# Projecting the next key and value ahead of the second pair's scores, in every unit of an attention stage

## The chip, the core and the metric

The kernel runs on one core of one Trainium2 chip. The metric is device time in microseconds (us) of one execution, from the kernel's start to its end. The kernel before takes 1142.35 us, the median of three runs (1141.11 to 1142.4).

## What is computed

Eight sequences of 128 tokens with 512 features each go through three small layers with residual sums (a linear layer with a low-rank adapter, a layer with a weight chosen for each sequence, a low-rank layer), and then through attention with 32 query heads and 8 key/value heads of size 128. A group of four query heads shares one key head. The keys are 512 cached rows, gathered through a page table, followed by the 128 new ones. The attention part, cut to what matters:

```python
q = rope(rmsnorm(x @ Wq.T, q_norm_w), pos)      # 32 heads of 128
k = rope(rmsnorm(x @ Wk.T, k_norm_w), pos)      # 8 heads of 128
v = x @ Wv.T
k_all = concatenate([k_cache[block_table], k])  # 512 + 128 keys
v_all = concatenate([v_cache[block_table], v])
scores = where(valid, (q @ k_all.T) * SCALE, -1e30)
o = softmax(scores) @ v_all
return x + o @ Wo.T
```

All of it is float32. Most products are made of three faster ones, high times high, high times low and low times high, so for most tiles there is a `_hi` and a `_lo` half.

## The kernel before

The first stage (about the first 120 us) does the three small layers. The second, which the change touches, has 64 **units**: unit u is one key/value head with one sequence, that is four query heads of 128 rows against 640 keys. Each engine has its own program, written by hand, in which `step(n, ...)` is what it does in round n. A loop runs over most rounds (`Fori`), and the first two and the last stand unrolled. There is no scheduler. An engine does its instructions in the order written and waits on semaphores (`wait_ge`).

Round n mixes three units:

- **TensorE** (PE; `step`, from L1060): the scores of heads 0 and 1 of unit n (`score_pair(n, 0)`, which waits for `qt_lo_out` and `kc_lo_out`), the queries of unit n+1 (`project_queries`, into ps_q), the scores of heads 2 and 3 (`score_pair(n, 1)`), the new key and value of unit n+1 (`project_new_key`, into ps_kv), the output product of unit n-2 (`put_out`), the turned cached keys of unit n+1 (`turn_cached`), its turned queries and new key (`turn_rotated`, which waits for `q_summed` and `key_scaled`), and the products with the values of unit n-1 (`values`, which waits for `pt_in`).
- **VectorE** (DVE; `step`, L1342): for each head the row minimum of the negated scores (`lowest`, line L1315, which waits for `scores`), then 1/sum (`inverse`), the turn of the probabilities in blocks of 32 (`turn_blocks`, L1339), and for unit n+1 the rotary products of the queries (`rotate_queries`, L1257 and L1262), the variances (`variances`, L1270, which waits for `sq_done` and `vn_out`), the rotated key (`rotate_key`, L1277 to L1282), and at the end the low halves (`cached_low`, `rotated_low`, L1236).
- **ScalarE** (ACT; `step`, L785): the exponentials (`exps`, L767), the scaling by 1/sum (`normalize`, L772), the squares of the next queries and key (`query_squares`, `key_squares`, L723), the next value's copy (`new_value`, L720 v_next), the scaled key (`scale_key`, L741, which waits for `key_summed` and for `rstd_done`), the high halves, and two of the four transfers that place the turned probabilities (`place_rest`, L280).
- **GpSimd** (POOL): it adds the query's two rotary products (`sum_queries`), raises the variances to the power -1/2 (`norm_factors`, L548), and gathers the next cached keys (L528 k_raw, once `turn_cached` is done) and values.
- **The queue of SyncE** (SP): it sends the turned probabilities of heads 0 and 1 and then those of heads 2 and 3 to memory (`send_blocks`, blocks_placed<-blocks), reads half of them back in another order (`place_rows`, prob_t<-blocks_placed), and loads the next input (`next_input`, x_s, which waits for `kv_proj`) and weights.

The probabilities thus go round a loop: turned on VectorE, sent by SP, placed by SP and ScalarE (`place_rest(n - 1)` stands in ScalarE's `step` ahead of `exps(n, 0)` and waits until both sends of unit n-1 have landed: `act.wait_ge(blocks_out, 32 * (n + 1))` in L775), and then used by `values`.

Of the kernel before, what the change touches and what calls it, by code (L numbers as in the profile page):

```python
# [50 lines left out]
def build(nc, x, x_t, ids0, ids1, ids2, table, lens, w0_t, bias0, lora_a, lora_b, w1_t, w2_b, w2_a,  # L51
          w_qkvo, q_norm, k_norm, k_rows, v_rows, inv_freq, row_in_table, ident_in, out):
    ctx = ExitStack()
    with ctx:
# [60 lines left out]
        with ExitStack() as p1:  # L115
# [81 lines left out]
            def one(t, at):  # L197

                return t[bass.ds(at, 1)].rearrange("a p k r -> p (a k) r") if len(t.shape) == 4 else t[bass.ds(at, 1)].rearrange("a p c -> (a p) c")
# [3 lines left out]
        with ExitStack() as p2:  # L203
# [94 lines left out]
            with nc.Block() as block:  # L298
# [308 lines left out]
                def _(act):  # L607
# [62 lines left out]
                    def store(e):  # L670
                        act.wait_ge(t3_lo, e + 1)
                        act.dma_start(one(xt_dram, e), x3t[:, :, :].bitcast(F32)).then_inc(xt_stored, 16)
# [60 lines left out]
                    def key_squares(u):  # L733
                        act.wait_ge(kv_proj, u + 1)
                        square(ps_kv[:, 0:D], GROUP)

                    def scale_key(u):

                        act.wait_ge(key_summed, u + 1)
                        act.wait_ge(rstd_done, u + 1)  # L740
                        nc.scalar.activation(rot[:, GROUP, :], key_sum[:, :], ACT.Copy, scale=rstd[:, GROUP:GROUP + 1]).then_inc(key_scaled, 1)  # L741
# [23 lines left out]
                    def exps(n, h):  # L765
                        act.wait_ge(low_done, GROUP * n + h + 1)
                        nc.scalar.activation(prob[:, h, :], prob[:, h, :], ACT.Exp, bias=low[:, h:h + 1], scale=-1.0,  # L767
                                             accum_out=total[:, h:h + 1]).then_inc(exp_done, 1)
# [16 lines left out]
                    def step(n, last, head=True, out=True, first=False, third=False):  # L785
                        if head:
                            out_high(n - 2, 1, first=first)
                        if out:
                            place_rest(n - 1, first=not head)
                        exps(n, 0)  # L790
                        exps(n, 1)
                        normalize(n, 0)
                        normalize(n, 1)
                        if not last:
                            query_squares(n + 1, range(GROUP))
                            key_squares(n + 1)
                            new_value(n + 1, first=not out)
                        if third:
                            third_turned(B - 1)
                            store(B - 1)  # L800
                        exps(n, 2)
                        exps(n, 3)
                        if not last:
                            scale_key(n + 1)
                        normalize(n, 2)
                        normalize(n, 3)
                        if not last:
                            cached_high(n + 1, first=not out)
                            rotated_high(n + 1)
                        if last:  # L810
                            keep_turned(0, 0, 1)
                            keep_turned(0, 2, 3)
                        if out:
                            out_high(n - 1, 0, first=not head)
# [26 lines left out]
                def _(pe):  # L841
# [105 lines left out]
                    def project_queries(u, first=False):  # L947
                        pe.wait_ge(x_s_in, 16 * (u + 1))
                        if not first:
                            pe.wait_ge(w_split, ((u >> 3) << 3) + B)  # L950
                            pe.wait_ge(qt_lo_out, u)
                        project(ps_q[:, :], u, 0, GROUP * D).then_inc(q_proj, 1)

                    def project_new_key(u, first=False):

                        if not first:
                            pe.wait_ge(vn_out, u)
                        project(ps_kv[:, 0:2 * D], u, GROUP * D, 2 * D).then_inc(kv_proj, 1)
# [16 lines left out]
                    def score_pair(n, pair):  # L975


                        pe.wait_ge(low_done, GROUP * n + 2 * pair)
                        heads = 2 * pair, 2 * pair + 1

                        def part(h, piece):
                            lo, hi = CUTS[h % 2][piece]
                            q = qt_hi[:, h * P:(h + 1) * P], qt_lo[:, h * P:(h + 1) * P]
                            return three(ps_s[:, score_slot(h) + lo:score_slot(h) + hi], q,
                                         (keys_of(kt_hi, n, lo, hi), keys_of(kt_lo, n, lo, hi)), True, True)

                        for h in heads:
                            part(h, 0)
                        for h in heads:
                            part(h, 1).then_inc(scores, 1)  # L990
# [69 lines left out]
                    def step(n, last, out=True, pv=True, third=False):  # L1060
                        pe.wait_ge(qt_lo_out, n + 1)
                        pe.wait_ge(kc_lo_out, n + 1)
                        score_pair(n, 0)
                        if third:
                            layer_2_out(B - 1, slot(B - 1))
                        if not last:
                            project_queries(n + 1)
                        score_pair(n, 1)
                        if third:
                            third_turn(B - 1)  # L1070
                        if not last:
                            project_new_key(n + 1)
                        if out:
                            put_out(n - 2)
                        if not last:
                            turn_cached(n + 1)
                            turn_rotated(n + 1)
                        if last:
                            turn_last(0)
                        if pv:  # L1080
                            values(n - 1, first=not out, beside=last)
# [37 lines left out]
                def _(dve):  # L1119
# [47 lines left out]
                    def keep_sum(e):  # L1167
                        dve.wait_ge(x3_out, e + 1)
                        nc.vector.tensor_copy(y[:, bass.ds(e, 1), :].rearrange("p a c -> p (a c)"), x3[:, :]).then_inc(y_out, 1)
# [172 lines left out]
                    def step(n, weights, last, head=True, out=True, first=False):  # L1342
                        if head:
                            out_low(n - 2, 1)
                        dve.wait_ge(mask_set, n + 1)
                        dve.wait_ge(gain_done, n + 1)
                        if not first:
                            dve.wait_ge(blocks_turned, GROUP * n)
                        lowest(n, 0)
                        lowest(n, 1)  # L1350
                        if weights:
                            weights_high(n)
                        inverse(n, 0)
                        inverse(n, 1)
                        if not last:
                            rotate_queries(n + 1)
                            rotate_queries_rest(n + 1)
                        if first:
                            third_sum(B - 1, slot(B - 1))
                            keep_sum(B - 1)  # L1360
                        lowest(n, 2)
                        lowest(n, 3)
                        if first:
                            third_turned(B - 1)
                        if not last:
                            turn_blocks(n, 0, first)
                            variances(n + 1)
                            rotate_key(n + 1)
                            turn_blocks(n, 1)
                        inverse(n, 2)  # L1370
                        inverse(n, 3)
                        if head:
                            add_out(n - 2)
                        if last:
                            keep_turned(0, 1, 2)
                        else:
                            turn_blocks(n, 2)
                            turn_blocks(n, 3)
                            cached_low(n + 1)
                            rotated_low(n + 1)  # L1380
                            gains(n + 1)
                        if out:
                            out_low(n - 1, 0)
                        if not last:
                            dve.wait_ge(low_done, GROUP * (n + 1))
                            set_mask(n + 1)
# [116 lines left out]
```

## Time and profile before

| | |
|---|---|
| time, median of 3 runs | 1142.35 us |
| lowest, highest | 1141.11, 1142.4 us |
| the profiled execution, its own time | 1145.5 us |
| its span, from first to last instruction | 1143.8 us |
| TensorE busy | 1109.5 us (97% of the span) |
| VectorE busy | 867.5 us (76%) |
| ScalarE busy | 697.3 us (61%) |
| GpSimd busy | 478.8 us (42%) |
| mean granted TensorE clock | 0.991 of full speed |

The profile is of one execution. Times of rows are us from the span's start, and durations of groups are means. TensorE's matmuls overlap, so the distance from one start to the next says what one costs. "[0.21 <-issue]" behind a row says that the engine sat idle for 0.21 us before it and waited for nothing that the profile shows; another name there is the instruction whose end released it. SPq, ACTq and POOLq are the engines as issuers of transfers.

### The profile page before, as it was taken

What the parts mean: (1) busy time and instruction counts of PE and PEld (TensorE: products, weight loads), DVE (VectorE), ACT (ScalarE), POOL (GpSimd) and SP (SyncE); (2) the same over time, 40 slices, a digit from 0 to 9 for tenths busy, and PEclk for the clock granted to TensorE, in tenths of its full rate; (3) what the DMA queues carried; (4) which work ended last, traced back from release to release, by engine and by line L of the source; (5) the groups of instructions that cost most, each with busy time, mean ns of one, the idle gap of its engine ahead of it and who ended that gap; (6) DMA issues with size and microseconds to landing.
All of it is one profiled execution on the core that took longest, in us unless ns stands there. A gap on an engine that the chain in (4) does not pass through costs nothing.

```text
span 1143.8 us, 27449 instructions
## 1 busy us (share of the span) xinstructions
PE 1109.5 (97%) x6116; PEld 972.0 (85%) x6116; DVE 867.5 (76%) x2203; ACT 697.3 (61%) x1949; POOL 478.8 (42%) x570
## 2 busy tenths in 40 slices
PE   5999699999999999999999999999999999999998
PEld 3656588888888889898898988989888888889886
DVE  3568778877787877778777887778877788777773
ACT  2344556766666666666666676666766666666663
POOL 6855334444344444344443444444444444432330
PEclk9999899999999999999999999999999999999999
DMA  6694577887778878787887887877888878777883
GB/s 180 211 310 164 176 233 252 260 256 242 256 246 270 254 235 259 246 273 248 243 255 247 266 251 249 252 255 252 259 252 246 255 254 264 234 222 227 245 249 99
DMA packets 125331, 275.77 MB, mean 241 GB/s; under 512 B 14076, under 2 KB 78716, under 8 KB 124290
## 3 DMA queue, kind: packets, MB, share of 16 engines
q1 hardware_dynamic: 78736, 193.37, 48.7%
q10 hardware_dynamic: 35426, 45.49, 16.1%
q0 software_dynamic: 11152, 36.72, 12.3%
q8 instruction: 6, 0.10, 0.0%
q14 instruction: 11, 0.09, 0.0%
HBM read 186.67 MB, written 88.87 MB: 241 GB/s over the span
## 4 chain that ended last, share of the span: by engine, by line
PE 85%; DMA 4%; DVE 1%; ACT 1%; issue 1%; POOL 0%; ACTq 0%; SPq 0%; DVEq 0%; POOLq 0%
PE ps_o L1008 23%; PE ps_q L943 15%; PE ps_kv L943 8%; PE ps_s L853 6%; PE ps_s L851 6%; PE ps_s L852 6%; PE ps_o L852 5%; PE ps_o L851 5%; PE ps_o L853 5%; DMA prob_t<-blocks_placed 2%; PE ps_q L972 2%; PE ps_x L964 2%; DMA blocks_placed<-blocks 2%; PE ps_kv L973 1%; DVE blocks L1339 1%
## 5 line engine op out<-in xcount | busy, mean ns | idle before, releaser
L767 ACT ACTIVATE prob<-prob,low 128x640 f32<-128x640 f32 x256 | 210.3, 827 | 156.8 <-DVE low L1315 148.3
L1315 DVE CUSTOM_DVE_ANT_0 prob<-ps_s,mask,q_gain 128x640 f32<-128x640 f32 x256 | 215.5, 879 | 34.3 <-PE ps_s L853 34.1
L1008 PE MATMUL ps_o<-prob_t,v_raw 128*128 128x256 f32 x992 | 236.0, 381 | 0.6 <-DMA prob_t<-blocks_placed 0.4
L1339 DVE STREAM_TRANSPOSE blocks<-prob 128x640 f32<-128x640 f32 x252 | 204.1, 829 | 1.8 <-ACT prob L772 1.8
L1008 PEld LDWEIGHTS ps_o<-prob_t,v_raw 128*128 128x128 f32 x992 | 184.5, 191 | 23.8 <-issue 1.0
L772 ACT ACTIVATE prob<-prob,inv 128x640 f32<-128x640 f32 x256 | 196.5, 815 | 0.0
L851 PE MATMUL ps_s<-kt_hi,qt_hi 128*128 (+1 forms) x512 | 171.1, 334 | 3.8 <-DVE kt_lo L1236 2.3
L943 PE MATMUL ps_q<-w_hi,x_s 128*128 (+1 forms) x512 | 171.5, 395 | 0.0
L853 PE MATMUL ps_s<-kt_hi,qt_lo 128*128 (+1 forms) x512 | 159.5, 311 | 0.0
L852 PE MATMUL ps_s<-kt_lo,qt_hi 128*128 (+1 forms) x512 | 159.0, 311 | 0.0
L720 ACT ACTIVATE ot_hi<-ps_o 128x256 fp32r<-128x256 f32 x128 | 49.0, 383 | 162.3 <-PE ps_o L1008 155.5
L108 POOL TENSOR_TENSOR w_lo<-w_raw,w_hi 128x640 f32 (+1 forms) x64 | 101.1, 1580 | 97.2 <-DVE w_hi L102 96.0
L1236 DVE TENSOR_TENSOR ot_lo<-ps_o,ot_hi 128x256 fp32r<-128x256 f32 x128 | 53.6, 419 | 84.5 <-ACT ot_hi L720 84.3
L544 POOL TENSOR_TENSOR rot<-rot_a,rot_b 128x512 f32<-128x512 f32 x64 | 82.8, 1293 | 81.6 <-DVE rot_b L1262 81.6
L943 PEld LDWEIGHTS ps_q<-w_hi,x_s 128*128 128x128 f32 x512 | 96.2, 188 | 20.7
L548 POOL TENSOR_TENSOR rstd<-var,neg_half 128x5 f32<-128x5 f32 x64 | 77.0, 1203 | 69.6 <-DVE var L1270 69.6
L851 PEld LDWEIGHTS ps_s<-kt_hi,qt_hi 128*128 128x128 f32 x512 | 96.9, 189 | 9.3 <-DVE kt_lo L1236 2.7
L943 PE MATMUL ps_q<-w_lo,x_s 128*128 (+1 forms) x256 | 101.1, 395 | 0.0
L852 PEld LDWEIGHTS ps_s<-kt_lo,qt_hi 128*128 128x128 f32 x512 | 97.1, 190 | 4.6
L943 PE MATMUL ps_kv<-w_hi,x_s 128*128 (+1 forms) x512 | 101.0, 281 | 0.0
L555 POOL COPY v_new<-v_next 128x128 f32 (+1 forms) x64 | 18.4, 288 | 192.7 <-PE ps_o L1008 177.2
L852 PE MATMUL ps_o<-w_lo,ot_hi 128*128 (+1 forms) x252 | 98.8, 392 | 0.0
(194 smaller groups left out, 2256.2 us busy)
## 6 DMA issues: line engine op xcount, KB each, us to landing
blocks_placed<-blocks SPq DMA_DIRECT2D x126, 640.0 KB, 3.9
prob_t<-blocks_placed ACTq DMA_DIRECT2D x126, 320.0 KB, 5.6
prob_t<-blocks_placed SPq DMA_DIRECT2D x126, 320.0 KB, 6.4
x_s<-xt_split SPq DMA_DIRECT2D x64, 512.0 KB, 3.7
w_raw<-w_qkvo_dram SPq DMA_DIRECT2D x55, 320.0 KB, 3.8
w<-w_t_dram SPq DMA_DIRECT2D x8, 1024.0 KB, 6.8
xt_split<-x3t ACTq DMA_DIRECT2D x8, 512.0 KB, 5.3
w_raw<-w_qkvo_dram POOLq DMA_DIRECT2D x9, 320.0 KB, 6.3
```

Of the source, the lines that this page charges most:

```text
L108: return nc.gpsimd.tensor_tensor(lo, raw, hi.bitcast(F32), ALU.subtract)
L544: nc.gpsimd.tensor_tensor(rot[:, 0:GROUP, :], rot_a[:, 0:GROUP, :], rot_b[:, 0:GROUP, :], ALU.add).then_inc(q_summed, 1)
L548: nc.gpsimd.tensor_tensor(rstd[:, :], var[:, :], neg_half[:, :], ALU.pow).then_inc(rstd_done, 1)
L767: nc.scalar.activation(prob[:, h, :], prob[:, h, :], ACT.Exp, bias=low[:, h:h + 1], scale=-1.0, accum_out=total[:, h:h + 1]).then_inc(exp_ ...
L772: nc.scalar.activation(prob[:, h, :], prob[:, h, :], ACT.Copy, scale=inv[:, h:h + 1]).then_inc(prob_done, 1)
L851: nc.tensor.matmul(dst, lh, rh, start=first, stop=False)
L852: nc.tensor.matmul(dst, lh, rl, start=False, stop=False)
L853: return nc.tensor.matmul(dst, ll, rh, start=False, stop=final)
L943: mm = nc.tensor.matmul(dst, x_s[:, int(i % 3 == 2), k * P:(k + 1) * P], w_rest if i % 3 == 1 else w, start=i == 0, stop=i == 3 * KT - 1)
L1008: mm = nc.tensor.matmul(ps_o[pair][:, 0:PAIR], v, turned_probs(c, pair), start=c == 0, stop=c == CH - 1)
L1315: nc.vector.tensor_tensor_reduce(out=prob[:, h, :], in0=ps_s[:, score_slot(h):score_slot(h) + KEYS], in1=mask[:, :], scale=q_gain[:, h:h + ...
L1339: nc.vector.transpose(blocks[:, h // 2, :, :, h % 2, :].rearrange("p j c q -> p c j q"), prob[:, h, :].rearrange("p (c j k) -> p c j k", c ...
```

## The change

No instruction is added or removed. In every unit that has a next one, three pieces move:

- TensorE: `project_new_key(n + 1)` stands ahead of `score_pair(n, 1)`, where it stood behind it.
- VectorE: `turn_blocks(n, 0)`, `variances(n + 1)` and `rotate_key(n + 1)` stand ahead of `lowest(n, 2)` and `lowest(n, 3)`.
- ScalarE: `scale_key(n + 1)` stands ahead of `exps(n, 2)` and `exps(n, 3)`.

```diff
@@ scalar, step @@
+                        if not last:
+                            scale_key(n + 1)
                         exps(n, 2)
                         exps(n, 3)
-                        if not last:
-                            scale_key(n + 1)
                         normalize(n, 2)
                         normalize(n, 3)
@@ tensor, step @@
                             project_queries(n + 1)
+                        if not last:
+                            project_new_key(n + 1)
                         score_pair(n, 1)
                         if third:
                             third_turn(B - 1)
-                        if not last:
-                            project_new_key(n + 1)
                         if out:
                             put_out(n - 2)
@@ vector, step @@
+                        if not last:
+                            turn_blocks(n, 0, first)
+                            variances(n + 1)
+                            rotate_key(n + 1)
                         lowest(n, 2)
                         lowest(n, 3)
                         if first:
                             third_turned(B - 1)
                         if not last:
-                            turn_blocks(n, 0, first)
-                            variances(n + 1)
-                            rotate_key(n + 1)
                             turn_blocks(n, 1)
                         inverse(n, 2)
                         inverse(n, 3)
```

VectorE's instructions in the middle of one unit (the second, which stands unrolled; the loop has the same order), from the rotary products of the queries on. The two pairs of ISA rows are `lowest` of heads 2 and 3. Before:

```order
L1257 TENSOR_TENSOR rot_a<-ps_q,cos_q 128x512
L1262 TENSOR_TENSOR rot_b<-ps_q,sin_q 128x4x64 x2
L1315 ISA prob,low<-ps_s,mask,q_gain 128x640
L1315 ISA low 128x1
L1315 ISA prob,low<-ps_s,mask,q_gain 128x640
L1315 ISA low 128x1
L1339 STREAM_TRANSPOSE blocks<-prob 128x5x4x32
L1270 TENSOR_SCALAR var<-sq 128x5
L1277 TENSOR_TENSOR rot_a<-ps_kv,cos_k 128x128
L1279 TENSOR_TENSOR rot_b<-ps_kv,sin_k 128x64 x2
L1282 TENSOR_TENSOR key_sum<-rot_a,rot_b 128x128
L1339 STREAM_TRANSPOSE blocks<-prob 128x5x4x32
```

And with the change:

```order
L1257 TENSOR_TENSOR rot_a<-ps_q,cos_q 128x512
L1262 TENSOR_TENSOR rot_b<-ps_q,sin_q 128x4x64 x2
L1339 STREAM_TRANSPOSE blocks<-prob 128x5x4x32
L1270 TENSOR_SCALAR var<-sq 128x5
L1277 TENSOR_TENSOR rot_a<-ps_kv,cos_k 128x128
L1279 TENSOR_TENSOR rot_b<-ps_kv,sin_k 128x64 x2
L1282 TENSOR_TENSOR key_sum<-rot_a,rot_b 128x128
L1315 ISA prob,low<-ps_s,mask,q_gain 128x640
L1315 ISA low 128x1
L1315 ISA prob,low<-ps_s,mask,q_gain 128x640
L1315 ISA low 128x1
L1339 STREAM_TRANSPOSE blocks<-prob 128x5x4x32
```

The transpose of head 0, the variances and the four instructions of the key moved from behind the two `lowest` to ahead of them.

ScalarE's instructions in the same unit, from the key's square to the scaling of heads 2 and 3; "x2" are the two heads. The difference, with - for before and + for the change:

```order
 L723 ACTIVATE junk,sq<-ps_kv 128x128
 L720 ACTIVATE v_next<-ps_kv 128x128
+L741 ACTIVATE rot<-key_sum,rstd 128x128
 L767 ACTIVATE prob,total<-prob,low 128x640 x2
-L741 ACTIVATE rot<-key_sum,rstd 128x128
 L772 ACTIVATE prob<-prob,inv 128x640 x2
```

The scaled key moved from behind the exponentials of heads 2 and 3 to ahead of them.

## Rows read from the trace of the kernel before

**Rows 1.** Busy time per stretch: stretch and length; PE, PEld, DVE, ACT, POOL; clock, DMA

```profile
608.09:623.89 15.80, 15.80 (x91) 14.19 (x90) 12.56 (x33) 10.21 (x29) 6.71 (x8) 1.00 0.80 249
200.00:1050.00 850.00, 850.00 (x4787) 762.79 (x4786) 675.97 (x1775) 550.96 (x1565) 353.79 (x425) 1.00 0.80 251
```

**Rows 2.** Timeline of TensorE, unit from 608.09: start us, us, engine, line, operation

```profile
612.84 0.28 PE L851 MATMUL ps_s<-kt_hi,qt_hi 128*128 x1
...
614.62 0.28 PE L943 MATMUL ps_kv<-w_hi,x_s 128*128 x1
```

**Rows 3.** Timeline of VectorE, the same unit

```profile
613.42 0.69 DVE L1257 TENSOR_TENSOR rot_a<-ps_q,cos_q 128x512 f32<-128x512 f32 x1 [0.21 <-issue]
614.02 0.74 DVE L1262 TENSOR_TENSOR rot_b<-ps_q,sin_q 128x256 f32<-128x256 f32 x2
614.69 0.87 DVE L1315 CUSTOM_DVE_ANT_0 prob<-ps_s,mask,q_gain 128x640 f32<-128x640 f32 x1
...
616.29 0.84 DVE L1339 STREAM_TRANSPOSE blocks<-prob 128x640 f32<-128x640 f32 x1
...
617.10 0.28 DVE L1277 TENSOR_TENSOR rot_a<-ps_kv,cos_k 128x128 f32<-128x128 f32 x1
...
617.67 0.29 DVE L1282 TENSOR_TENSOR key_sum<-rot_a,rot_b 128x128 f32<-128x128 f32 x1
...
619.17 0.69 DVE L1332 TENSOR_TENSOR y<-ps_o,y 128x512 f32 x1 [0.34 <-PE ps_o L853]
619.78 1.56 DVE L1339 STREAM_TRANSPOSE blocks<-prob 128x640 f32<-128x640 f32 x2
...
622.43 0.27 DVE L1236 TENSOR_TENSOR kt_lo<-ps_kv,kt_hi 128x128 f32 x1
```

**Rows 4.** Timeline of ScalarE, the same unit

```profile
610.30 0.85 ACTq L280 DMA_DIRECT2D prob_t<-blocks_placed  x2
...
614.88 0.28 ACT L723 ACTIVATE junk<-ps_q 128x128 f32<-128x128 f32 x1 [0.42 <-DVE rot_b L1262]
...
616.24 0.28 ACT L723 ACTIVATE junk<-ps_kv 128x128 f32<-128x128 f32 x1 [0.21 <-PE ps_kv L943]
...
616.50 0.27 ACT L720 ACTIVATE v_next<-ps_kv 128x128 f32 x1
616.66 0.83 ACT L767 ACTIVATE prob<-prob,low 128x640 f32<-128x640 f32 x1
...
617.47 0.83 ACT L767 ACTIVATE prob<-prob,low 128x640 f32<-128x640 f32 x1
...
618.87 1.53 ACT L772 ACTIVATE prob<-prob,inv 128x640 f32<-128x640 f32 x2
```

**Rows 5.** Timeline, POOL and ACTq, same unit; then transfers issued from 621.1 to 621.6

```profile
617.26 1.20 POOL L548 TENSOR_TENSOR rstd<-var,neg_half 128x5 f32<-128x5 f32 x1 [1.03 <-DVE var L1270]
...
620.64 1.05 POOL L528 DMA_INDIRECT k_raw<-k_rows_dram,k_row  x1 [0.79 <-POOL k_row L525]
...
626.19 0.85 ACTq L280 DMA_DIRECT2D prob_t<-blocks_placed  x2
...
blocks_placed<-blocks SPq DMA_DIRECT2D x1, 640.0 KB, 4.7
```

**Rows 6.** Unit 1: key gather, second send, and that send's us to landing

```profile
143.49 1.05 POOL L528 DMA_INDIRECT k_raw<-k_rows_dram,k_row  x1 [0.79 <-POOL k_row L525]
...
145.45 0.33 SPq L275 DMA_DIRECT2D blocks_placed<-blocks  x1
...
blocks_placed<-blocks SPq DMA_DIRECT2D x1, 640.0 KB, 3.7
```

**Rows 7.** Transfers issued from 998.1 to 998.5, us to landing last: a first send

```profile
blocks_placed<-blocks SPq DMA_DIRECT2D x1, 640.0 KB, 3.0
```

**Rows 8.** Timeline of TensorE and VectorE, unit from 892.66: scores begin; queries are rotated

```profile
892.66 0.47 PE L851 MATMUL ps_s<-kt_hi,qt_hi 128*128 x1
...
897.81 0.69 DVE L1257 TENSOR_TENSOR rot_a<-ps_q,cos_q 128x512 f32<-128x512 f32 x1 [0.56 <-PE ps_q L943]
```

## The prediction, made before the changed kernel ran

> **What bounds the kernel now.** Read the busy time by stretch first [rows 1]. From 200 to 1050 us TensorE is busy for all of the 850 us, at the full granted clock, and VectorE for 676. The unit that I follow starts its scores at 608.09 and the next at 623.89. It is 15.80 us long, and TensorE is busy for all of it. The 18 units from there to 892.66 [rows 8] give 15.81 us each. So TensorE sets the time, and an order that lets the others be ready sooner can give nothing back there. The question is only whether TensorE is made to wait. That is read from the timelines of the other engines, as the distance from their last step to TensorE's need.
>
> Two such distances matter. The first: VectorE ends the last low half, which `score_pair(n+1, 0)` waits for, at 622.43 + 0.27 = 622.70 [rows 3], and TensorE needs it at 623.89, so 1.19 us are to spare. The second is less visible. ScalarE issues `place_rest` at 610.30 [rows 4] and at 626.19 [rows 5], each time when the second send of the unit before has landed, and its first exponential of the unit stands behind that issue. From these exponentials come the inverses of heads 0 and 1, and `rotate_queries` stands behind those on VectorE: it starts at 613.42, 3.12 us after the issue, and its 0.21 us of idleness before has no release by TensorE [rows 3]. So a loop runs through ScalarE, VectorE and a transfer: place, exponentials, queries rotated, ... head 3 turned, sent, landed, place. The loop is kept in step by TensorE at one point only: the square of the key waits 0.21 us for `project_new_key` [rows 4].
>
> **The change part by part.** I count from R, the start of `rotate_queries`, and put each later step beside what it was.
>
> TensorE: the same matmuls in another order. The scores of the second pair take 614.62 - 612.84 = 1.78 us [rows 2], so the key and value are ready 1.78 us sooner, and the second pair's scores later by the shorter key projection. By itself that costs TensorE nothing. The key's square no longer waits. It then follows the query squares, which is 0.2 to 0.35 us sooner, because those began at R + 1.46 and did not move [rows 4]: I take R + 2.5, before R + 2.82. The one point at which TensorE kept the loop in step is gone.
>
> VectorE: after the query rotation it turns head 0 (0.84 us) and is then early. `variances` waits for the copy of the value, which ScalarE makes behind the squares: R + 2.5 + 0.26 + 0.27 = R + 3.03 [rows 4]. Behind this wait stand the key's rotation and now both `lowest`. After a short wait the register work of a dynamic address shows, as 0.21 us did for the queries [rows 3], so the key's rotation starts at R + 3.24, its sum 0.57 us later [rows 3] and `lowest(n, 2)` about 0.2 us behind that, at R + 4.0. Before, it was at 614.69, which is R + 1.27. **The second pair's minima start 2.7 us later**; the scores are there long before.
>
> ScalarE: `lowest` takes 0.87 and its result is read just behind, so `exps(n, 2)` starts at R + 4.93 where it was at 616.66, R + 3.24. The new order on ScalarE gives about the same moment by another way: GpSimd's power starts 0.16 us after the key's rotation (617.10 to 617.26) and takes 1.20 us [rows 3, 5], so to R + 4.6, and the scaled key comes between it and the exponential, some 0.4 us. So `scale_key` ahead of the exponentials adds next to nothing more. 1.7 us are lost here, since before the exponential had waited for the squares anyhow. Then: `exps(n, 3)` 0.81 later at R + 5.74; the scaling of head 2 at R + 6.6 and of head 3 at R + 7.36, ended at R + 8.17 (before 618.87 + 1.53, R + 6.98) [rows 4].
>
> VectorE again: `inverse(n, 3)` waits for the exponential of head 3, to R + 6.7, and behind it stands `add_out`, with some 0.3 us of instruction and registers ahead of it: R + 7.0. From there 0.61 to the transposes and 1.56 for both [rows 3]: **head 3 is turned at R + 9.17**, before 621.34, R + 7.92. The last low half ends 622.70 - 621.34 = 1.36 later, R + 10.53, and TensorE can start at R + 10.65 with the 0.12 us that ScalarE needs after VectorE's end (614.76 to 614.88). Before it started at R + 10.47. Against an R that does not move that is 0.18 us too late.
>
> Two lengths follow. **TensorE and VectorE alone:** R cannot be sooner than 5.15 us after the unit's first score, which is where it starts when it does wait for TensorE (892.66 to 897.81) [rows 8]. 5.15 + 10.65 = 15.80: just what a unit is now. **The loop through the transfer:** 3.12 from place to R, 9.17 to head 3 turned, L for the send's landing, and 0.15 for the steps at its two ends (626.19 - 621.34 - 4.7), together 12.44 + L. At L = 4.7 as now [rows 5] that is 17.14. The same steps before are 626.19 - 610.30 = 15.89, with the key's wait of 0.21 among them: without the wait 15.68, so the loop was just under a unit's length.
>
> **What L will be** is the one unknown. The second send shares the transfer engines with the gather of the cached keys, issued at 620.64, 0.7 us before head 3 is turned (621.34), and lands in 4.7 us [rows 5]. In unit 1 the gather was issued 145.45 - 143.49 = 1.96 us ahead of the send, and it landed in 3.7 [rows 6]. A send with nothing beside it lands in 3.0 [rows 7]. Both ends are kept: 3.0 gives 15.44, which is under TensorE's own 15.80, and 4.7 gives 17.14. The gather hangs on TensorE's turn, 620.64 - 608.09 = 12.55 us after the unit's first score. With a unit of 16.14 us the place is issued 16.14 - 3.12 - 10.65 = 2.37 after the first score and the second send 3.12 + 9.17 + 0.07 after that, at 14.7: 2.2 us behind the gather. That is nearest to rows 6, so I take L = 3.7, and the unit is **16.14 us**.
>
> The Trainium skill ("DMA: Bandwidth & Descriptors", Anatomy of one DMA) gives a transfer about 2.0 us fixed and its bytes over 436 GB/s, which for 640 KB is an estimate of 3.5 us; by it the unit would be 15.94 and the kernel 1150 us. The trace disagrees for a send alone: 3.0 [rows 7].
>
> The sum: units 2 to 61 run in this loop, 60 of them. 60 x (16.14 - 15.81) = 19.8 us. Against the profiled execution's own 1145.5 us that is 1165; against the median of the runs, 1142.35, it is 1162. What the other side gives is small: the wait of `turn_rotated` for the key scaled falls away, at most the 0.01 us by which 15.81 is over 15.80, 0.6 us in all. `next_input` and the next weights are issued some 1.8 us sooner, while the probabilities are being placed. SP's own two placements stand ahead of them in its queue, so I take nothing; if they did delay the last placement, that would be in the upper part of the range.
>
> **Rivals.**
> 1. *Not slower: the send has the engines to itself.* If L is 3.3 or less, 12.44 + L is under 15.8, the loop has slack again, and R falls back to 5.15, at which the other length is 15.80. Then the time is 1142 (1140 to 1144). For it: the gather is moved 1.5 us further ahead of the send, and 3.0 was seen [rows 7]. Against it: the first send now goes out beside the gather and both push work toward the second, and in rows 6 1.96 us were not enough.
> 2. *The send lands in 3.3 to 3.6 us.* Unit 15.8 to 16.04, time 1143 to 1156. This is where the skill's figure, DMA: Bandwidth & Descriptors, would put it.
> 3. *L stays 4.4 to 4.7.* The unit is 16.84 to 17.14 us, the time 60 x 1.03 to 1.33 more, 1204 to 1222. For it: nearly every unit of the trace shows it. Against it: each shows it at the same distance from the gather, which the change moves.
> 4. *Faster*: only if waits at TensorE that I priced at 0.6 us were larger. Nothing in rows 1 allows it.
>
> **How the numbers follow.** Forecast, L of 3.6 to 4.3 and a time of 1156 to 1200: 0.45, likeliest 1162. Rival 1: 0.21. Rival 2: 0.16. Rival 3: 0.12. Rival 4: 0.03. The remaining 0.03 are slower in a way I do not name. A measurement of this kernel can tell about 0.2% (2.3 us) from no change. So slower has 0.76, the same 0.21 and faster 0.03. The range from 1142 to 1200 holds the forecast, rival 2 and most of rival 1, about 8 in 10, and leaves out rival 3.
>
> **What would show it.** In the profile after, units are 16.0 to 16.4 us apart, and TensorE has a gap before the scores of each (ps_s L851, released by kt_lo L1236), where before it had none. `lowest(n, 2)` starts 4.0 us after `rotate_queries` instead of 1.27, with about 1 us of idle VectorE ahead of the variances, released by v_next. The first exponential of a unit still follows the place issue directly, and the second send lands in 3.6 to 4.3 us. Wrong would be: no gap ahead of the scores and a second send of about 3.0 us (rival 1), or a chain from R to the last low half that is not near 10.5 us.

## The result, and the profile with the change

The kernel with the change takes **1154.47 us** (median of six runs, 1151.77 to 1158.59). The kernel before took 1142.38 us beside it (median of six, 1141.11 to 1143.85). The ratio is 1.0111, with a 95% interval of 1.0091 to 1.0131, so it is 1.1% slower. The profiled execution took 1158.59 us, the longest of the six, with a span of 1156.9 us.

Times below are medians, and "unit" is the distance from one unit's first score to the next, between 200 and 1050 us. Before it is 15.81 us in 49 of 52 units. Now 44 of 52 are 15.96 to 16.00, the median is 15.97, four take 16.20 to 16.28, and the mean is 16.00. 60 units by 0.19 are 11.4 us, nearly all of the 12.1 us.

Busy time of one typical unit and of the long stretch; the columns are those of [rows 1], which it answers:

```profile
615.56:631.53 15.97, 15.97 (x91) 14.06 (x90) 12.85 (x35) 10.00 (x29) 6.69 (x8) 1.00 0.79 249
200.00:1050.00 850.00, 849.09 (x4730) 747.47 (x4731) 680.15 (x1749) 530.23 (x1538) 351.31 (x424) 1.00 0.78 248
```

By the busy time TensorE still looks full, since the record of a matmul is longer than the distance to the next start. The last one of the products with the values starts at 631.21 and is shown for 0.38 us, over the whole gap ahead of the next scores. The wait shows in the idle time of the weight load ahead of the scores (20.0 us in 54 units, in the list of waits below, where the kernel before has none) and in the distances between starts. The timeline of TensorE in the same unit (first score; first key and value matmul; scores of the second pair; the last two matmuls of the values; the next unit's first score):

```profile
615.56 0.38 PE L851 MATMUL ps_s<-kt_hi,qt_hi 128*128 x1
...
620.22 0.28 PE L943 MATMUL ps_kv<-w_hi,x_s 128*128 x1
...
621.59 0.28 PE L851 MATMUL ps_s<-kt_hi,qt_hi 128*128 x1
...
630.99 0.59 PE L1008 MATMUL ps_o<-prob_t,v_new 128*128 128x256 f32 x2
631.53 0.38 PE L851 MATMUL ps_s<-kt_hi,qt_hi 128*128 x1
```

VectorE in that unit, answering [rows 3]. The number behind "idle" in brackets is the idle time just before the row:

```profile
620.62 0.69 DVE L1257 TENSOR_TENSOR rot_a<-ps_q,cos_q 128x512 f32<-128x512 f32 x1 [0.27 <-PE ps_q L943]
...
621.89 0.83 DVE L1339 STREAM_TRANSPOSE blocks<-prob 128x640 f32<-128x640 f32 x1
623.74 0.17 DVE L1270 TENSOR_SCALAR var<-sq 128x5 f32<-128x5 f32 x1 [1.01 <-ACT junk L723]
623.87 0.29 DVE L1277 TENSOR_TENSOR rot_a<-ps_kv,cos_k 128x128 f32<-128x128 f32 x1
...
624.67 0.88 DVE L1315 CUSTOM_DVE_ANT_0 prob<-ps_s,mask,q_gain 128x640 f32<-128x640 f32 x1
...
628.25 1.56 DVE L1339 STREAM_TRANSPOSE blocks<-prob 128x640 f32<-128x640 f32 x2
...
630.90 0.28 DVE L1236 TENSOR_TENSOR kt_lo<-ps_kv,kt_hi 128x128 f32 x1
```

ScalarE, answering [rows 4]: the placement, the key's square, the scaled key, and the exponential and the scaling of the second pair:

```profile
617.45 0.85 ACTq L280 DMA_DIRECT2D prob_t<-blocks_placed  x2
...
623.10 0.29 ACT L723 ACTIVATE junk<-ps_kv 128x128 f32<-128x128 f32 x1
...
625.28 0.40 ACT L741 ACTIVATE rot<-key_sum,rstd 128x128 f32<-128x128 f32 x1 [1.64 <-POOL rstd L548]
625.59 0.82 ACT L767 ACTIVATE prob<-prob,low 128x640 f32<-128x640 f32 x1
...
627.23 1.53 ACT L772 ACTIVATE prob<-prob,inv 128x640 f32<-128x640 f32 x2
```

The cached keys' gather, the second send and the placement behind it, answering [rows 5, 6]; they come from the timelines of POOL, SP and ACTq:

```profile
627.98 1.05 POOL L528 DMA_INDIRECT k_raw<-k_rows_dram,k_row  x1 [0.79 <-POOL k_row L525]
...
629.89 0.33 SPq L275 DMA_DIRECT2D blocks_placed<-blocks  x1
...
633.46 0.86 ACTq L280 DMA_DIRECT2D prob_t<-blocks_placed  x2
```

And what the engines waited for from 200 to 1050 us (us in total, times, longest):

```profile
ACT rot L741 <- POOL rstd L548: 86.8, 53, 1.6
...
DVE var L1270 <- ACT junk L723: 53.9, 53, 1.0
...
PEld ps_s L851 <- issue: 20.0, 54, 0.7
DVE rot_a L1257 <- PE ps_q L943: 12.8, 45, 0.4
```

Two things are to be seen. The first is a new idle microsecond of VectorE ahead of the variances, in each of 53 units, with both minima behind it. The second is the line on ps_q: in 45 of 53 units the rotation of the queries now waits for TensorE, where before it did so in 12. A TensorE that starts its unit late is itself what starts the next long chain late.

### The profile page after: what moved, and what is told of

Same layout as the page of the kernel before. It is cut to its first block and busy times, and to the rows that moved or that the text cites. A ratio compares the mean times of both kernels' runs of the same rounds, so it can differ in the third digit from the quotient of the medians.

```text
span 1156.9 us, 27449 instructions
## 1 busy us (share of the span) xinstructions
PE 1118.7 (97%) x6116; PEld 964.2 (83%) x6116; DVE 885.9 (77%) x2203; ACT 684.7 (59%) x1949; POOL 480.0 (41%) x570
## 5 line engine op out<-in xcount | busy, mean ns | idle before, releaser
L851 PE MATMUL ps_s<-kt_hi,qt_hi 128*128 (+1 forms) x512 | 165.9, 324 | 7.1 <-DVE kt_lo L1236 4.5
L853 PE MATMUL ps_o<-w_hi,ot_lo 128*128 (+1 forms) x252 | 99.5, 395 | 0.0
L943 PE MATMUL ps_kv<-w_hi,x_s 128*128 (+1 forms) x512 | 98.3, 277 | 0.0
L851 PE MATMUL ps_o<-w_hi,ot_hi 128*128 (+1 forms) x252 | 98.1, 389 | 0.0
```

Source lines behind the costliest of these rows:

```text
L851: nc.tensor.matmul(dst, lh, rh, start=first, stop=False)
L853: return nc.tensor.matmul(dst, ll, rh, start=False, stop=final)
L943: mm = nc.tensor.matmul(dst, x_s[:, int(i % 3 == 2), k * P:(k + 1) * P], w_rest if i % 3 == 1 else w, start=i == 0, stop=i == 3 * KT - 1)
```

## The experiments

The distances between the first matmuls of TensorE's pieces tell where a unit is lost. They are medians between 200 and 1050 us, and each ends at the next piece in the order of that kernel. "Scores" without a number are those of heads 0 and 1, "scores 2" those of heads 2 and 3.

| us | before | after | key scaled last | TensorE alone | TensorE undone | one minimum first |
|---|---|---|---|---|---|---|
| scores to queries | 1.946 | 1.860 | 1.946 | 1.946 | 1.858 | 1.946 |
| queries | 2.800 | 2.800 | 2.800 | 2.800 | 2.800 | 2.800 |
| key and value | 1.413 | 1.372 | 1.372 | 1.372 | 1.413 | 1.372 |
| scores 2 | 1.787 | 1.766 | 1.766 | 1.766 | 1.787 | 1.766 |
| output product | 2.748 | 2.764 | 2.764 | 2.764 | 2.748 | 2.764 |
| turned cached keys, to turned queries | 0.435 | 0.435 | **1.635** | **1.446** | 0.435 | 0.435 |
| turned queries and key, to values | 0.546 | 0.546 | 0.573 | 0.574 | 0.546 | 0.546 |
| values, to next scores | 4.132 | **4.426** | 4.132 | 4.132 | **4.879** | 4.132 |
| mean unit | 15.81 | 16.00 | 16.99 | 16.80 | 16.48 | 15.77 |

### Each part alone

**The scaled key put back behind the exponentials**, with the rest of the change kept:

```diff
-if not last:
-    scale_key(n + 1)
 exps(n, 2)
 exps(n, 3)
+if not last:
+    scale_key(n + 1)
```

> The changed kernel with ScalarE's part alone undone: scale_key stands behind exps(n, 2) and exps(n, 3) again. Theory A (the chain behind the wait for the value's copy, and each engine's place in it, sets the unit): the exponentials do not start sooner, since the minima are not ready before 10.0 us after the unit's first score; the scaled key comes behind them, at about 12.0 instead of 10.1, and turn_rotated on TensorE, which needs it at 11.0, waits for it: unit about 16.9 us, time about 1205 (1190 to 1215). Rival (VectorE's new order alone costs time, ScalarE's place is neutral): 1154, as with the change.

It took 1215.76 us, 1.0647 (1.062 to 1.0674) of the kernel before. The size of theory A was right to 1%, the time just above its range. TensorE's turned queries wait, since the new key that is turned with them comes last on ScalarE:

```profile
620.12 0.39 ACT L741 ACTIVATE rot<-key_sum,rstd 128x128 f32<-128x128 f32 x1
...
620.65 0.63 PE L972 MATMUL ps_q<-ident,rot 128*128 128x128 f32 x4 [1.04 <-ACT rot L741]
```

So the third part of the change is what makes the second one bearable: it is worth some 60 us here.

**TensorE's part alone** on the kernel before:

```diff
+if not last:
+    project_new_key(n + 1)
 score_pair(n, 1)
 if third:
     third_turn(B - 1)
-if not last:
-    project_new_key(n + 1)
```

> The kernel before with TensorE's part alone: project_new_key ahead of score_pair(n, 1), VectorE and ScalarE as before. Theory A: the scores of heads 2 and 3 come 1.4 us later, lowest(n, 2) waits for them to 7.7 us after the first score instead of 6.6, and all that stands behind it, the variances and the key among it, is 1.1 us later; the scaled key is ready at 12.0 where turn_rotated needs it at 11.1: unit about 16.9 us, time about 1207 (1190 to 1215). Rival (a move among matmuls on an engine that is always busy costs nothing by itself, as the prediction said): 1142.

It took 1200.28 us, 1.0513 (1.0486 to 1.0541). The rows of VectorE, POOL, ScalarE and TensorE in one unit:

```profile
622.54 0.88 DVE L1315 CUSTOM_DVE_ANT_0 prob<-ps_s,mask,q_gain 128x640 f32<-128x640 f32 x1 [1.17 <-PE ps_s L853]
...
625.13 1.21 POOL L548 TENSOR_TENSOR rstd<-var,neg_half 128x5 f32<-128x5 f32 x1 [2.31 <-DVE var L1270]
...
626.43 0.40 ACT L741 ACTIVATE rot<-key_sum,rstd 128x128 f32<-128x128 f32 x1 [1.22 <-POOL rstd L548]
...
626.97 0.41 PE L972 MATMUL ps_q<-ident,rot 128*128 128x128 f32 x2 [0.85 <-ACT rot L741]
```

The minima wait for scores that now come 1.4 us later, and in the old order the variances stand behind them, and so on through GpSimd and ScalarE to TensorE. The sentence "by itself that costs TensorE nothing" in the prediction is wrong when the part stands alone: 1.0 us in each unit.

**TensorE's part undone**, with VectorE's and ScalarE's kept:

```diff
-if not last:
-    project_new_key(n + 1)
 score_pair(n, 1)
 if third:
     third_turn(B - 1)
+if not last:
+    project_new_key(n + 1)
```

> The changed kernel with TensorE's part alone undone: project_new_key stands behind score_pair(n, 1) again, VectorE and ScalarE as with the change. Theory A: the key's square waits for TensorE to 8.06 us after the first score instead of starting at 7.54, the value's copy and all behind it are 0.52 us later, so the unit grows from about 15.97 to about 16.5: time about 1184 (1176 to 1192). Rival (the loop through the transfer sets the unit, and VectorE's chain has slack): less than 0.1 us a unit, 1154 to 1160.

It took 1183.23 us, 1.037 (1.0342 to 1.0398), as theory A had it. VectorE's wait ahead of the variances is 1.52 us long instead of 1.01, and what is late at the end is the last low half, as a gap ahead of the scores:

```profile
616.46 0.17 DVE L1270 TENSOR_SCALAR var<-sq 128x5 f32<-128x5 f32 x1 [1.52 <-ACT junk L723]
...
624.24 0.38 PE L851 MATMUL ps_s<-kt_hi,qt_hi 128*128 x1 [0.40 <-DVE kt_lo L1236]
```

0.51 us more of this one wait made the median unit 0.50 us longer (16.47 against 15.97). That is the clearest evidence that the wait lies on the chain that sets the time.

### The wait filled

One `lowest` put into VectorE's idle microsecond, and one exponential into ScalarE's:

```diff
@@ vector @@
 turn_blocks(n, 0, first)
+lowest(n, 2)
 variances(n + 1)
 rotate_key(n + 1)
-lowest(n, 2)
 lowest(n, 3)
@@ scalar @@
-if not last:
-    scale_key(n + 1)
 exps(n, 2)
+if not last:
+    scale_key(n + 1)
 exps(n, 3)
```

> The changed kernel with lowest(n, 2) moved into VectorE's idle time, between turn_blocks(n, 0) and variances(n + 1), and scale_key between exps(n, 2) and exps(n, 3). Nothing else differs. Theory A (the loss is the wait for the value's copy with both minima queued behind it): head 2's minimum is taken while the copy is made, head 3 is turned near 13.6 us after the first score instead of 14.25, the last low half ends near 15.0 and TensorE does not wait: unit 15.80, time 1142 (1140 to 1145). Rival (the loop through the transfer sets the unit, since the second send again goes out close behind the gather of keys): 15.9 to 16.1, 1147 to 1158.

It took 1138.88 us (median of twelve), 0.998 (0.9961 to 1.0) of the kernel before, and 1.3% less than the change. VectorE waits 0.33 us for the scores and then not at all for the squares:

```profile
617.82:633.58 15.76, 15.76 (x91) 14.13 (x90) 12.78 (x34) 10.22 (x29) 6.69 (x8) 1.00 0.81 256
...
625.85 0.88 DVE L1315 CUSTOM_DVE_ANT_0 prob<-ps_s,mask,q_gain 128x640 f32<-128x640 f32 x1 [0.33 <-PE ps_s L853]
...
626.66 0.17 DVE L1270 TENSOR_SCALAR var<-sq 128x5 f32<-128x5 f32 x1
```

So taking one of the two minima out from behind the wait, with its exponential ahead of the scaled key, gives the whole loss back. The two moves were made together, and neither was tried alone. TensorE does not wait any more, and its unit is 15.76 us, 0.05 shorter than before. The table says why: key and value right behind the queries cost 0.041 us less, the second scores 0.021 less, the output product 0.016 more. 60 units by 0.05 are 3 us. Measured were 2.4 us against the kernel before beside it, in an interval that reaches from none to 4.5, so the gain in time is no more than likely. I had expected no gain (15.80).

### Which of two loops sets the unit

The prediction had two lengths: the chain through TensorE and VectorE, and the loop through the transfer. In the changed kernel the first is 15.97. For the second the typical unit has 12.44 + 3.43, which is 15.87, too near to tell them apart by the lengths. The start of the query rotation tells more. Where nothing else holds it, it follows the placement by 3.11 us. In 38 of 52 units it comes later than that, 3.13 to 3.30 us behind the placement, since VectorE waits for TensorE's queries there, and these units are set by the chain through TensorE. In the other 14 the placement is the last to come, or ties. The transfer loop passes ScalarE only because the placements stand ahead of its exponentials. If SP issues all four, it is cut. One wait had to be added to ScalarE's end, for all sends, ahead of the copies of the last unit's turned probabilities:

```diff
@@ sync, step @@
-for j in range(NB // 2):
+for j in range(NB):
     place_rows(sp, j)
@@ scalar, step @@
-if out:
-    place_rest(n - 1, first=not head)
@@ scalar, keep_turned @@
+act.wait_ge(blocks_out, 32 * (UNITS - 1))
```

> The changed kernel with all four placements of the turned probabilities issued by SP; ScalarE issues none, so its first exponential no longer stands behind the landing of the second send, and the loop through the transfer is cut. Theory A (the chain of TensorE, VectorE and ScalarE sets nearly every unit, 15.97 us, and the transfer only the few whose send is late): those few go, mean unit 16.00 to 15.97, time 1151 to 1154. Rival (the loop through the transfer sets the unit): it falls to 15.80 or near, time 1142 to 1146.

It took 1160.87 us, 1.0176 (1.0158 to 1.0195): both missed, theory A by 7 us. The waits from 200 to 1050 us:

```profile
DVE rot_a L1256 <- PE ps_q L942: 29.8, 53, 0.6
PEld ps_s L850 <- issue: 13.4, 40, 0.6
...
PEld ps_o L1007 <- issue: 4.7, 14, 0.6
PE ps_o L1007 <- DMA prob_t<-blocks_placed: 1.5, 5, 0.4
```

The queries' rotation now waits for TensorE in all 53 units, so the transfer loop is off it, and still 40 units have the gap ahead of the scores, with the median unit at 15.99. But SP's last two placements come later and the products with the values wait for them, a cost that the experiment added.

The same was then tried with the placements left on ScalarE, but behind the exponentials of heads 0 and 1:

```diff
-if out:
-    place_rest(n - 1, first=not head)
 exps(n, 0)
 exps(n, 1)
+if out:
+    place_rest(n - 1, first=not head)
```

> The changed kernel, with ScalarE's two placements of the turned probabilities issued behind the exponentials of heads 0 and 1 instead of ahead of them. The loop through the transfer then no longer passes through the exponentials, and has over 1 us to spare. Theory A (the chain TensorE and VectorE alone, 5.06 + 10.56 + 0.35 us, sets the unit): the typical unit stays 15.97 us, only the units with a late send get as short as the others, time 1152 (1150 to 1155). Rival (the loop through the transfer sets the unit, the gap ahead of the scores is only where it shows): the unit falls to 15.80 us, time 1142 to 1145. The placements are issued at 2.9 and 3.3 us after the unit's first score and land 6 us later, 1.5 us or more ahead of the products with the values.

It took 1160.23 us, 1.0165 (1.0132 to 1.0197). The time is out of both ranges. The units decide nevertheless: with the transfer loop cut, none is shorter than 15.96, and 19 of 52 are 15.96 or 15.97. The rival, 15.80, did not come about in a single unit. So the chain through TensorE and VectorE gives 15.97, and what is over it here is late placements again: the products with the values start 0.617 us on average behind the turned queries, where 0.546 is the undisturbed distance.

### The hidden loop in the kernel before

If the transfer loop was just under a unit before, a small copy on ScalarE, idle 39% of the time, must cost something when it stands in that loop. It adds a copy of 128x512 ahead of the unit's first exponential; nothing reads what it writes:

```diff
 if out:
     place_rest(n - 1, first=not head)
+copy(junk[:, 0:GROUP, :].rearrange("p h d -> p (h d)"), pos[:, :])
 exps(n, 0)
```

> The kernel before with one extra instruction a unit on ScalarE, a copy of 128x512 into a scratch tile, behind place_rest and ahead of exps(n, 0), about 0.5 us. ScalarE is busy for 61% of the time and TensorE for 97%. Theory A (a hidden loop through ScalarE, VectorE and the transfer runs just under the unit's length): the copy lengthens the way from the placement to rotate_queries by 0.5 us, the scaled key comes too late for turn_rotated, unit 15.9 to 16.25, time about 1157 (1148 to 1169). Rival (ScalarE has room): 1142.

It took 1155.19 us, 1.0127 (1.0104 to 1.015), theory A to 2 us. The mean unit is 15.99, and what waits is the turned queries, for the scaled key:

```profile
PEld ps_q L973 <- issue: 8.9, 29, 0.5
...
PE ps_q L973 <- ACT rot L741: 1.7, 8, 0.3
```

The copy lengthens the way from the placement to the rotation by 0.45 us (3.56 against 3.11). Some of it comes back, as the second send is now 0.98 us behind the gather and lands in 4.39 us instead of 4.56.

To show that its place in the loop is what costs, the loop was cut for it in the two ways from above. With SP issuing all placements:

> The kernel before with the same extra copy, and with all four placements issued by SP. Theory A: without the placement ahead of it the copy lies in ScalarE's idle time before the first minimum is ready (2.6 us after the first score), and the time is 1142 (1140 to 1145). Rival (the copy costs by itself, wherever the placement is): as the run before it.

It took 1157.84 us, 1.0132 (1.0109 to 1.0156). And with ScalarE's placements behind the exponentials:

> The kernel before with the same extra copy on ScalarE ahead of the unit's first exponential, and the two placements behind the exponentials of heads 0 and 1. Theory A (the extra copy cost 0.18 us a unit only because it stands in the loop through the transfer): unit back to 15.81 us, time 1142 (1140 to 1145). Rival (the copy costs by its time on ScalarE, wherever the placements stand): unit 15.99, time 1155 as with the copy alone.

It took 1162.86 us, 1.0169 (1.0133 to 1.0206). Both expectations missed. The waits of TensorE for the values' operand, first of the one, then of the other:

```profile
PEld ps_o L1008 <- issue: 12.1, 28, 0.7
PE ps_o L1008 <- DMA prob_t<-blocks_placed: 4.9, 16, 0.4
```

```profile
PEld ps_o L1009 <- issue: 11.5, 27, 1.1
PE ps_o L1009 <- DMA prob_t<-blocks_placed: 5.0, 13, 0.9
```

In both the wait of the turned queries is gone: their distance is back at 0.435 us in every unit, from 0.59 on average with the copy alone, and 15 of 52 units of the second are at 15.81. So the wait that the copy had caused does come through the loop. The time shows no gain, since each cut moved the wait to the values. What the placements behind the exponentials cost in the kernel before without the copy was not run, so the times of these two runs can't be split between the copy and the later placements. In the second, ScalarE's placements are issued 1.4 us later, at 3.6 instead of 2.2 us after the unit's first score, and also take longer, 7.0 us to landing where they took 5.9 before. The issues from 200 to 1050 us, of this kernel and then of the kernel before:

```profile
prob_t<-blocks_placed ACTq DMA_DIRECT2D x106, 320.0 KB, 7.0
```

```profile
prob_t<-blocks_placed ACTq DMA_DIRECT2D x107, 320.0 KB, 5.9
```

At the same time SP's own placements, which did not move in the second, land in 5.1 us where they took 6.7.

The last run gave the version with one minimum ahead the same later placements:

> The version with one minimum ahead of the variances, and the two placements behind the exponentials of heads 0 and 1. Theory A (TensorE was already busy for all of the unit there, 15.76 us): no change, 1139 (1137 to 1141). Rival (some units still lose to late sends): mean unit 15.75 instead of 15.77, time 1137 to 1138.

It took 1165.86 us, 1.0207 (1.0177 to 1.0237), where 1139 was expected: 27 us more than with the placements in their old position, and only those moved. Its waits:

```profile
PEld ps_o L1008 <- issue: 19.2, 38, 1.5
PE ps_o L1008 <- DMA prob_t<-blocks_placed: 9.8, 21, 1.2
```

So this kernel has a third limit that I had not reckoned with, in the prediction or here: the placements must be issued as soon as the second send has landed. Why a later issue also lengthens the landing was not tried. They then run beside other transfers of the unit, and which of these costs them the time is open.

## Why the prediction was right, and where its sizes were off

The prediction was 1162 us, with 1142 to 1200 as its range, and "slower" at 0.76. The time was 1154.47: slower, by 12.1 us where 19.8 were forecast. It lies 1.5 us under the band of 1156 to 1200 that the prediction held likeliest. That the number came this near is in part luck, as the two errors of size below have opposite signs.

- **The mechanism.** The chain of the changed order held step by step. From R, the start of the query rotation at 620.62, the key's square comes at 2.48 (2.5 predicted), the key's rotation at 3.25 (3.24), the first of the second pair's minima at 4.05 (4.0), its exponential at 4.97 (4.93), its scaling at 6.61 (6.6), head 3 turned at 9.19 (9.17), and the last low half ends at 10.56 (10.53). VectorE idles 1.0 us ahead of the variances, as it said, though the profile names the key's square as the release. The value's copy, for which it also waits, ends at 623.65, 0.09 us ahead of the variances.
- **TensorE's wake was mis-sized.** The step "TensorE can start at R + 10.65 with the 0.12 us that ScalarE needs after VectorE's end" took one engine's delay for another's. From the end of the last low half at 631.18 to the first score at 631.53 are 0.35 us, in nearly every unit of the change, and in every one with TensorE's part undone. The gap is where the prediction wanted it, but between 200 and 1050 us the profile calls it "issue" and does not name kt_lo, as it does with TensorE's part undone.
- **R** can be a little sooner than 5.15: 5.06, because the first scores take 1.86 instead of 1.95 us when TensorE has waited ahead of them. Without the wait the first one's record begins while the last matmul of the values still runs, and is 0.47 us long [rows 8] instead of 0.38. With both, the chain is 5.06 + 10.56 + 0.35, or 15.97 instead of 15.80, and it is longer than TensorE's own work. The prediction held this chain for just as long as a unit and put the whole loss on the other. That is the step that was wrong about the mechanism: the loop that it named as the bound sets at most 14 of 52 units.
- **L, the landing of the second send,** was 3.43 (3.32 to 3.79, from send to placement less 0.1 us), not 3.7. In the rows above it is 633.46 - 629.89 - 0.1, or 3.47. It was issued 1.91 us behind the gather. The prediction reckoned with 2.2 us behind the gather, and took 3.7 from [rows 6], where the distance is 1.96. The transfer loop is therefore 15.87 and not 16.14, and sets only the units whose send lands late, as when the place comes at 2.17 us after the first score and the unit is 16.23. L was in the range of rival 2, and the time with it. The bound of most units was in none of the four.
- **The two errors partly cancelled.** By the prediction's own sum, L of 3.43 alone gives 1146 (60 by 0.06 us); the chain of 15.97 gives 60 by 0.16, or 9.6 us, and the late sends some 2 us more. That makes 1154.
- **Weighed against the skill's figure.** The second send took 3.43 us beside the gather. The Trainium skill ("DMA: Bandwidth & Descriptors", Anatomy of one DMA) gives an estimate of 3.5 for its bytes, and at this distance the trace is near it. The page's figures are a fit of transfers that GpSimd issues, and this one is issued by SP. At 0.78 us behind the gather, as before, it was 4.56, at 1.29 us (one minimum ahead) 3.93, and alone 3.0 [rows 7]. So the agreement holds at one distance and not at the others.
- **"By itself that costs TensorE nothing"** is true inside this change and false alone, as the second experiment shows. What the earlier projection gives inside it is 0.50 us a unit (the third).

## What to carry to other kernels

An instruction that waits holds back all that stands behind it on its engine: before moving one ahead, put beside its wait the work that will be queued there, and place as much of it ahead as fits in the wait. Add up each loop that closes through several engines, with the delay between them measured on the engine that wakes, since an engine that is busy all the time hides loops that are hardly shorter than its own work: here 15.68 against 15.80 us. To cut a loop by moving a transfer's issue tests less than it seems, as the transfer may have no slack of its own.

## What the hardware showed that I had not expected

- TensorE, released by VectorE ahead of the scores, starts 0.35 us after the end of the releasing instruction, where ScalarE followed VectorE by 0.12 in the kernel before (614.76 to 614.88). Three of TensorE's register instructions stand between the release and the weight load: the trace has them 0.31, 0.21 and 0.12 us ahead of the first score. That they are the difference was not tried.
- The same matmuls take 0.046 us less in a unit in another order: the key and value 1.372 instead of 1.413 us when they follow the queries, which use the same x_s. It was the same in all kernels with that order. That the shared x_s is the reason was not tried.
- The landing of one transfer of 640 KB changes with how long ago the gather was issued: 4.56, 4.39, 3.93 and 3.43 us at 0.78, 0.98, 1.29 and 1.91 us. That is not the whole of it: with TensorE's part alone it is 3.62 at 1.85 us, and with TensorE's part undone 3.44 at 2.36. No run moved the gather by itself.
- A wait of TensorE can be absent from its busy time: between 200 and 1050 us the change loses 10 us of work, and busy time falls by only 0.9. The record of the matmul before the gap lasts 0.38 us, and the next start comes 0.32 us after its own.
